# Last stage of a graph network kernel: TensorE adds x, ScalarE takes the sum out of PSUM and scales it

## What is computed

```python
x = _layernorm(x + _L0_gnn_ref(x, edge_index, ...))      # kept in the table x1_tab
# _L1_gnn_ref, 4 heads of 32:
alpha = ex / (denom[dst] + 1e-16)
agg = jax.ops.segment_sum(vj * alpha[:, :, None], dst, num_segments=n)
out = agg.reshape(n, HID) + (x @ Wskip + bskip)
h = jax.nn.gelu(out @ W1 + b1, approximate=True)
h = jax.nn.gelu(h @ W2 + b2, approximate=True)
x = _layernorm(x + (out + h))                            # the result
```

## Time and profile before

| | us |
|---|---|
| median of 3 runs (6085.18 to 6090.76) | 6087.27 |
| profiled execution | 6087.56 |
| its span | 6085.8 |
| PE busy | 5029.0 (83%) |
| DVE busy | 4721.2 (78%) |
| POOL busy | 3935.9 (65%) |
| ACT busy | 2815.7 (46%) |

### The profile page before, as it was taken

The page is one execution under the profiler, slowest core; times in us unless marked ns, Lnnn a source line. Parts: engine busy times, 40 slices in busy tenths (PEclk is TensorE's granted clock), DMA queues, the critical chain, the costliest instruction groups (busy, mean ns, idle before and its releaser), DMA issues. The chain is left out here.

```text
span 6085.8 us, 103985 instructions
## 1 busy us (share of the span) xinstructions
PE 5029.0 (83%) x26752; PEld 4077.5 (67%) x26752; DVE 4721.2 (78%) x14274; ACT 2815.7 (46%) x8831; POOL 3935.9 (65%) x3976
## 2 busy tenths in 40 slices
PE   7499999998798769966699778976698869877765
PEld 3389999997687448843488447854487658666654
DVE  8577777776687657878787886879887879888886
ACT  7167777775465653322233332333232237644442
POOL 1377777777665875556555875567666866466664
PEclk9699999998899989989899998999897569989998
DMA  0289988875466879989898998989997556444332
GB/s 2 54 230 264 262 264 260 248 246 175 149 205 191 263 241 313 322 295 345 301 322 299 320 332 289 323 317 383 319 286 214 176 150 172 143 125 124 124 120 78
DMA packets 930909, 1406.71 MB, mean 231 GB/s; under 512 B 157981, under 2 KB 453981, under 8 KB 930355
## 3 DMA queue, kind: packets, MB, share of 16 engines
q1 hardware_dynamic: 650867, 872.50, 44.6%
q0 software_dynamic: 138368, 296.57, 17.5%
q10 hardware_dynamic: 141120, 231.27, 10.1%
HBM read 827.23 MB, written 572.88 MB: 230 GB/s over the span
## 5 line engine op out<-in xcount | busy, mean ns | idle before, releaser
L1388 DVE SCALAR_TENSOR_TENSOR c_rows<-bank,carry,c_rows 32x256 f32<-32x256 f32 (+2 forms) x1950 | 889.5, 456 | 562.0 <-PE bank L1990 262.7
L1756 PE MATMUL bank<-c_rows,sums_all 128*128 128x256 f32 (+1 forms) x1960 | 736.4, 463 | 435.0 <-DVE c_rows L1388 417.6
L1396 POOL DMA_INDIRECT c_rows<-t_tab,src_pair x784 | 741.0, 945 | 519.8 <-PE bank L1990 360.6
L1396 POOL DMA_INDIRECT c_rows<-y_tab,src_pair x784 | 789.2, 1007 | 382.7 <-issue 170.5
L1756 PEld LDWEIGHTS bank<-c_rows,sums_all 128*128 128x128 f32 x1960 | 344.9, 221 | 817.4 <-DVE c_rows L1388 800.7
L1775 ACT ACTIVATE c_squares<-c_y,c_root 128x256 f32<-128x256 f32 x784 | 391.8, 500 | 803.5 <-DVE c_y L1865 392.1
L2033 ACT ACTIVATE c_xt<-bank 128x512 f32<-128x512 f32 x392 | 234.0, 597 | 905.0 <-PE bank L1999 905.0
L1753 PE MATMUL bank<-bias_rows,c_degs 128*128 128x256 f32 (+1 forms) x1960 | 621.6, 405 | 27.3 <-DMA c_degs<-kap_tab 27.3
L749 PE MATMUL bank<-w_mix,lxt 128*128 128x256 f32 x2400 | 611.2, 383 | 1.4 <-ACT lxt L1026 1.4
L749 PE MATMUL bank<-w_mix,c_xt 128*128 128x256 f32 x2352 | 606.2, 381 | 0.0
L750 PE MATMUL bank<-bias_rows,two_r 128*128 128x256 f32 (+1 forms) x1400 | 593.4, 426 | 0.0
(11 more groups left out here) (388 smaller groups left out, 12953.5 us busy)
## 6 DMA issues: line engine op xcount, KB each, us to landing
y_tab<-ly SPq DMA_DIRECT2D x400, 256.0 KB
t_tab<-lt SPq DMA_DIRECT2D x400, 256.0 KB
c_own<-y_tab SPq DMA_DIRECT2D x392, 256.0 KB
t_tab<-c_y ACTq DMA_DIRECT2D x392, 256.0 KB
c_own<-t_tab SPq DMA_DIRECT2D x392, 256.0 KB
c_z<-y_tab SPq DMA_DIRECT2D x294, 256.0 KB
y_tab<-c_y ACTq DMA_DIRECT2D x294, 256.0 KB
c_z<-t_tab SPq DMA_DIRECT2D x294, 256.0 KB
```

The source lines that it names most:

```text
L1388: nc.vector.scalar_tensor_tensor(rows, before[p0:p0 + 32, :], m["carry"][p0:p0 + 32, t:t + 1], rows, ALU.mult, ALU.add).then_inc(S["carrie ...
L1396: pool.indirect_dma_start(out=two(m["c_rows"], j % 4, H2)[:, i, 0:w], out_offset=None, in_=source, in_offset=bass.IndirectOffsetOnAxis(ap= ...
L1756: nc.tensor.matmul(out, sums[:, 2 * j + i, :], two(rows, j % 4, H2)[:, i, 0:w], start=False, stop=True).then_inc(S["summed"], 1)
```

## The change

`both`, `add`, `far_again` and `x_again` go. `back` adds three things in PSUM, each by a matmul with the identity as moving operand, which also turns it: `skip`, `down` and the turned x itself. For that `xt` becomes a ring of eight. ACT takes the sum out of PSUM (`settle`) and does the last scaling (`apply`) as `inverse * y + shift`; DVE only makes `shift` = -mean * inverse for two pairs at once.

```diff
-        xt = sb("fl_xt", [P, 2, 2 * P])
+        xt = sb("fl_xt", [P, 8, 2 * P])
-        both = sb("fl_sum", [P, 2, 2 * P])
+        shifts = sb("fl_shift", [P, 4, 2])
@@ SP
-                                 (BEGIN - 4, every, load), (5, each, far_again)])
+                                 (BEGIN - 4, every, load)])
@@ PE
                 def back(j):
-                    pe.wait_ge(S["sum"], fp.at("sum", j))
+                    pe.wait_ge(S["down_set"], fp.at("down_set", j))
                     if j >= 2:
                         pe.wait_ge(S["y"], fp.at("y", j - 2))
                     for i in range(2):
-                        last = nc.tensor.transpose(psum[6 + j % 2][:, i * P:(i + 1) * P],
-                                                   both[:, j % 2, i * P:(i + 1) * P], ident[:])
+                        out_ = psum[6 + j % 2][:, i * P:(i + 1) * P]
+                        nc.tensor.matmul(out_, skip[:, j % 4, i * P:(i + 1) * P], ident[:], start=True, stop=False)
+                        last = nc.tensor.matmul(out_, down[:, j % 2, i * P:(i + 1) * P], ident[:], start=False, stop=False)
+                        last = nc.tensor.matmul(out_, xt[:, j % 8, i * P:(i + 1) * P], ident[:], start=False, stop=True)
                     last.then_inc(S["back"], 1)
@@ ACT
                 def copy(j):
                     act.wait_ge(S["turned"], fp.at("turned", j))
-                    if j >= 2:
-                        act.wait_ge(S["skip"], fp.at("skip", j - 2))
+                    if j >= 8:
+                        act.wait_ge(S["back"], fp.at("back", j - 8))
...
+                def settle(j):
+                    s = j % 4
+                    act.wait_ge(S["back"], fp.at("back", j))
+                    if j >= 4:
+                        act.wait_ge(S[f"scattered{s}"], fp.ring_at("scattered", j, s, back=1))
+                    nc.scalar.activation(y[:, s, :, :].rearrange("p i c -> p (i c)"), psum[6 + s % 2][:, 0:2 * P], ACT.Copy
+                                         ).then_inc(S["y"], 1)
+
+                def apply_both(j):
+                    if j % 2:
+                        apply(j - 1)
+                        apply(j)
+
+                def apply(j):
+                    s = j % 4
+                    act.wait_ge(S["shifted"], fp.at("shifted", j))
+                    for i in range(2):
+                        last = nc.scalar.activation(y[:, s, i, :], y[:, s, i, :], ACT.Identity,
+                                                    bias=shifts[:, s, i:i + 1], scale=inverse[:, s, i:i + 1])
+                    last.then_inc(S["done"], 1)
+                in_turns(total, [(6, each, settle), (0, each, copy), (1, 1, line_copy), (1, each, skip_), (2, each, up_), (3, each, down_),
+                                 (7, each, apply_both), (18, 1, weight)])
@@ DVE: add, the first part of norm, scale_both and scale go; new:
+                def shift_both(j):
+                    if j % 2:
+                        dve.wait_ge(S["inverse"], fp.at("inverse", j))
+                        s = (j - 1) % 4
+                        v.scalar_tensor_tensor(shifts[:, s:s + 2, :], mv[:, s:s + 2, :, 0], -1.0,
+                                               inverse[:, s:s + 2, :], ALU.mult, ALU.mult).then_inc(S["shifted"], 2)
...
-                                 (BEGIN + 2, every, carry_on(0)), (7, each, scale_both),
+                                 (BEGIN + 2, every, carry_on(0)), (7, each, shift_both),
                                  (BEGIN + 5, every, divide), (6, each, norm), (BEGIN + 3, every, carry_on(1)),
-                                 (4, each, add), (BEGIN + 1, every, weigh)])
+                                 (BEGIN + 1, every, weigh)])
```

More of the change, by code:

```diff
@@ L2408, in shares_and_finish @@
     v, psum, ident = nc.vector, m["psum"], m["ident"]
-    fp = counts.phase(finish, {"far_in*": 16, "others_in*": 16, "turned": 1,
+    fp = counts.phase(finish, {"far_in*": 16, "turned": 1,
                             "copied": 1, "skip": 1, "skip_set": 1, "up": 1, "up_set": 1, "down": 1,
-                            "down_set": 1, "sum": 1, "back": 1, "y": 1, "stats": 2, "var": 1,
+                            "down_set": 1, "back": 1, "shifted": 1, "y": 1, "stats": 2, "var": 1,
                             "inverse": 1, "done": 1, "scattered*": 32})
@@ L2446, in shares_and_finish @@
         x_in = sb("fl_x", [P, 4, 2, D])
-        x_again = sb("fl_x2", [P, 4, 2, D])
-        xt = sb("fl_xt", [P, 2, 2 * P])
+        xt = sb("fl_xt", [P, 8, 2 * P])
         skip = sb("fl_skip", [P, 4, 2 * P])
@@ L2599, in skip_ @@
                     c = order[j]
-                    last = nc.tensor.matmul(psum[3][:, 0:2 * P], m["w_skip"][:], xt[:, j % 2, :],
+                    last = nc.tensor.matmul(psum[3][:, 0:2 * P], m["w_skip"][:], xt[:, j % 8, :],
                                             start=True, stop=c >= pairs)
@@ L2649, in copy @@
                     act.wait_ge(S["turned"], fp.at("turned", j))
-                    if j >= 2:
-                        act.wait_ge(S["skip"], fp.at("skip", j - 2))
-                    nc.scalar.activation(xt[:, j % 2, :], psum[2][:, 0:2 * P], ACT.Copy
+                    if j >= 8:
+                        act.wait_ge(S["back"], fp.at("back", j - 8))
+                    nc.scalar.activation(xt[:, j % 8, :], psum[2][:, 0:2 * P], ACT.Copy
                                          ).then_inc(S["copied"], 1)
@@ L2657, in skip_ @@
                     if j >= 4:
-                        act.wait_ge(S["sum"], fp.at("sum", j - 4))
+                        act.wait_ge(S["back"], fp.at("back", j - 4))
                     nc.scalar.activation(skip[:, j % 4, :], psum[3][:, 0:2 * P], ACT.Identity,
@@ L2671, in down_ @@
                     if j >= 2:
-                        act.wait_ge(S["sum"], fp.at("sum", j - 2))
+                        act.wait_ge(S["back"], fp.at("back", j - 2))
                     nc.scalar.activation(down[:, j % 2, :], psum[5][:, 0:2 * P], ACT.Gelu_apprx_tanh,
                                          bias=m["b_down"][:]).then_inc(S["down_set"], 1)
-                in_turns(total, [(0, each, copy), (1, 1, line_copy), (1, each, skip_), (2, each, up_), (3, each, down_),
-                                 (18, 1, weight)])
+                def settle(j):
[18 more added lines that the diff above has]
+                                 (7, each, apply_both), (18, 1, weight)])
             @block.vector
@@ L2816, in divide @@
                     last.then_inc(S["shared"], 1)
[L2818 to L2823, removed]
                 def norm(j):
                     s = j % 4
[L2827 to L2832, removed]
                     dve.wait_ge(S["y"], fp.at("y", j))
@@ L2842, in norm @@
                     v.tensor_scalar(var[:, s, :], mv[:, s, :, 1], LN_EPS, None, ALU.add).then_inc(S["var"], 1)
-                def scale_both(j):
+                def shift_both(j):
                     if j % 2:
[L2846 to L2855, removed]
+                        dve.wait_ge(S["inverse"], fp.at("inverse", j))
+                        s = (j - 1) % 4
+                        v.scalar_tensor_tensor(shifts[:, s:s + 2, :], mv[:, s:s + 2, :, 0], -1.0,
+                                               inverse[:, s:s + 2, :], ALU.mult, ALU.mult).then_inc(S["shifted"], 2)
                 in_turns(total, [(1, 1, line_copy), (3, 1, gates), (6, 1, blocks(0)), (7, 1, to_row(0)),
```

## The result

| | before | after |
|---|---|---|
| median of 4 runs, us | 6086.23 (6082.52 to 6090.76) | 6524.43 (6518.28 to 6529.75) |
| span of the profiled execution | 6085.8 | 6528.0 |
| its granted clock, mean | 0.914 | 0.900 |
| POOL's inverse 0, 6, 86, 95, 98 at | 5293.9, 5342.2, 5944.4, 6048.6, 6070.8 | 5294.3, 5358.8, 6370.1, 6488.1, 6512.5 |
| cycle of the middle (inverse 6 to 86, by 80) | 7.53 | 12.64 |

The account below looks back on a forecast made before the run. It took POOL's round trip to bound the middle and DVE's order the pairs-only stretch. A new loop of 8.40 us gives +69.5, pairs only +15: +84.5 on 6087.27, 6172 us, 1.4% slower; forecast 6140 to 6205 (0.62).

Parts of the forecast that it names:

- the sentence on rings: Slot waits of `copy`, `skip_` and `down_` on `back`: all at least two pairs old, costed at nothing.
- so I take its clock as full: PE in the middle: at a cycle of 8.40 it waits once, 1.64 us against 1.83, so full clock.
- The middle: Stretch of coupled and far pairs: 80 cycles of 8.40 us, 672.0 instead of 602.5, so +69.5 us.
- The new loop: Middle: one pass per cycle through ACT's `apply` and `settle`, DVE's `norm` and carry, PE's two turns; 8.40 us.
- `settle` waiting for a scatter: ACT's wait for a scatter of four pairs ago: landing has 3.9 us, costed at nothing; seeing it would count as wrong.
- Pairs only: Stretch behind the middle: two-turn cycle 12.68 us at full clock, 13.2 at 0.85; nine cycles, +15 us.
- The head: Before 5342 us, far pairs without carries: stays with POOL, 7.35 against 7.39, costed at nothing.
- The clock rival: Middle: the granted clock falls there too, costing +38 to +67 us, about 6225 us; chance 0.15.
- POOL's round trip: Middle before: inverse to DVE's scalings and back, a 1.45 us wait, no slack in POOL's 7.39 us cycle.
- PE "has slack": Middle before: PE waits 1.83 us per cycle in front of `add_up(1)` for the carry of DVE.
- POOL's own start: First scatter starts 0.28 or 0.8 us after its release, making POOL's cycle 7.35 or 7.87; 7.35 by the skill's rule.

Follow-up runs that it names:

- e1: The changed kernel with a ring of eight for `skip` and four for `down`, nothing else; 6186.13 us, 1.0161 times before.
- e5: The changed kernel with eight small matmuls that nobody reads in PE's wait in front of `add_up(1)`; 6384.69 us.
- e2: The changed kernel with only the ring of `skip` made eight long, `down` left at two; 6416.99 us.
- e7: The kernel before with only the last scaling moved: `shift` on DVE, `apply` on ACT; 6229.59 us.
- e8: The kernel before with a ring of eight for y, scaling one turn later and scatters behind the next inverse; 6083.89 us, 1.0002 times before.

## Why the prediction was wrong, point by point

**The step that failed** is the sentence on rings: "`copy` now waits for `back` of eight pairs ago, `skip_` and `down_` for `back` instead of the sum; all are at least two pairs old. I cost it at nothing." The age was counted in pairs and not in turns. Pair j-4 is four pairs old, but `back` stands four turns behind `skip_`, so it is of the same turn, and the last thing in it. The sum, at start 4, was of the turn before. Subtracting the starts, 5 - 4 = 1 for `skip_` and 5 - 2 = 3 for `down_`, against their own 1 and 3, would have shown it without any trace. What the runs show in place of that nothing: PE and ACT in series, 480.8 of 800 us of waiting in front of `skip_`, and 338 us that two longer rings give back. The rest of the forecast is close for a kernel with longer rings: 6172 forecast, 6186 in e1.

The second step to fall, as a consequence, is "so I take its clock as full". It rested on a wait of 1.64 us in front of `add_up(1)`; with the series the wait was 2.7 and the clock 0.81.

**The middle**, forecast +69.5, measured +409.1. Each step is a difference of measured cycles, times 80:

| from | to | us per cycle | us |
|---|---|---|---|
| before 7.53 | e1 8.55: the forecast's loop | 1.02 | 82 |
| e1 8.55 | e5 10.81: ring waits, full clock | 2.26 | 181 |
| e5 10.81 | after 12.64: lower clock level | 1.83 | 146 |

**The new loop** was right where the ring waits are away: 8.40 forecast, 8.2 in e1's plain cycles and 8.55 in the mean. Some of what the mean has above 8.2 is `settle` waiting for a scatter, which had been costed at nothing: 36.1 us in 76 cycles, 0.47 each, in 18 of them. The terms held: 1.53 from `apply` to `settle` (1.58), 1.34 for `back`'s twelve passes at the full clock (1.32), 0.40 to the statistics (0.42). These lines of e1 show the last two and that `apply` follows `down_` in ACT's own order, without a wait for `shift`:

```profile
5708.59 0.38 PE L2622 MATMUL bank<-ident,fl_skip 128*128 128x128 f32 x2
...
5708.80 0.47 ACT L2668 ACTIVATE fl_down<-bank,b_down 128x256 f32<-128x256 f32 x1
...
5709.17 1.64 ACT L2687 ACTIVATE fl_y<-fl_y,fl_shift,fl_inv 128x128 f32<-128x128 f32 x4
...
5709.93 0.38 PE L2584 MATMUL bank<-ident,fl_x 128*128 128x128 f32 x2
...
5710.70 0.36 ACT L2675 ACTIVATE fl_y<-bank 128x256 f32<-128x256 f32 x1
5710.84 1.03 POOL L2528 DMA_INDIRECT out_dram<-fl_y,node_of  x1 [3.89 <-ACT fl_y L2687]
...
5711.10 0.49 DVE L2837 BATCH_NORM_STATS2 fl_stats<-fl_y 128x6 f32<-128x128 f32 x2 [1.77 <-ACT fl_y L2675]
```

**Pairs only**: 13.2 per cycle forecast, 13.11 measured, +13.8 us for +15. It was met because this stretch escapes the failed step: neighbouring pairs are two turns apart, so four pairs are eight turns and `back` of pair j-4 is long done. The two halves of the cycle from 6411.79 to 6425.28 are 6.67 with the inverse (6.72 forecast) and 6.82 with `apply` (5.96 forecast, at the full clock); in the second `down_` took 0.86, its time at the lower clock level. So the clock's part came in the half without the inverse and was larger there than the 0.5 that had been forecast for both; the sum fits better than its halves, and to that extent it was luck. From 6380 to 6480 us `skip_` waits for its own matmul alone:

```profile
ACT fl_skip L2654 <- PE bank L2598: 10.7, 15, 0.9
```

**The head**: +16.2 where nothing was forecast. Far pairs come one per turn there, so the same ring wait holds; e1, without it, has 51.4 us from inverse 0 to 6, before 48.4, after 64.5.

**The clock rival** was no rival but an addition. What the forecast held against it, that PE's busy share rises from 73% to 80%, didn't come: PE is busy 74% of the middle, at the lower clock, and its work at the full clock, 6.76 by the forecast's own count, is 53% of a cycle of 12.64. The longer wait in front of `add_up(1)` goes with the lower clock, as the rival had it, though not in strict order: 1.5 us and a clock of 0.98 in e1, 1.83 and 0.90 before, 2.7 and 0.81 after, 2.7 and 0.83 in e2, 3.0 and 0.84 in e7. That the idle time brings the clock down, e5 alone shows, by filling it.

**What bounded the kernel before** was only half seen. POOL's round trip had no slack, as the rows said, but e8 took its wait away and gained nothing in the middle: a second loop of about the same length lay behind it. That PE "has slack" and that POOL's cycle "has no slack" were both read from waits, and a wait shows who came last, not by how much.

**POOL's own start.** The forecast left open whether a scatter needs 0.28 or 0.8 behind its release. It is 0.8 with no DVE scaling beside it: in the changed kernel `apply` starts at 5810.18, two take 0.88, and the scatter starts at 5811.86, 0.80 later; in e1 it is 5709.17 and 5710.84, 0.79. DVE stands idle in both stretches. The Trainium skill ("SBUF — State Buffer", section "Who interferes with whom") would have put it down to VectorE's `tensor_scalar` holding the shared port pair; here none runs and the 0.8 stays, so that rule does not explain it. The trace does show what lies in it: POOL's queue has a MOVE for each of these scatters, the first 0.03 to 0.04 after the second scaling has ended and 0.77 ahead of the scatter (5811.09 in the changed kernel). Both figures are the medians of all 99 cycles, and the same in before, after, e1 and e7. The gather of the earlier trace rows has no MOVE; its wait record lies at 5151.63, 0.23 ahead of it. Of all indirect DMAs of the kernel before only those written with `bounds_check` have one, 398 of 398, and none of the others. That leaving the check out would save the difference is not shown; no run tried it. The start decided nothing in the changed kernel, whose cycle is far above either value.

## What to carry to other kernels

When a wait is moved from one step to another, or a buffer gets a later reader, subtract: the start of the step that frees the slot, less the ring's length, against the start of the step that waits. If the result is the same turn, two engines that worked beside each other work in turn, and by the same subtraction the ring has to grow by at least the number of turns that the reader moved (one here; the runs tried 8 for 4 and 4 for 2 only). Look then at what the new wait does to PE's clock: here the idle time that the series made cost another 1.83 us per cycle. And before shortening one loop look for the next one behind it.

## What the runs showed of the hardware

- Idle time of PE in front of `add_up(1)` cost more than work in its place: eight matmuls that nobody reads, put into a wait of 2.7 us per cycle, raised the granted clock of the middle from 0.81 to 1.00 and took 1.83 us off each cycle of 12.64.
- A f32 pass of 128 columns against the identity was 0.11 us at the full clock and 0.21 at the lower level (5819.80 to 5821.13 for twelve, granted clock 1.00, and 5814.95 to 5817.51, granted clock 0.50).
- The first indirect scatter of a cycle starts about 0.8 us after the scaling that releases it, whether that ran on ACT with DVE idle (after, e1) or on DVE with two more scalings beside it (before); 0.77 of it lie between a MOVE in POOL's queue and the scatter. A gather without such a MOVE, released by PE, started 0.28 after that matmul's end as the profile models it.
